# Conditional residual layer on one core: the first transfers, the slot table, the bias tiles and two weight loads change places

## The reference

```
selected_W = W[cat_ids]
selected_b = b[cat_ids]
out = x + jnp.einsum('bsd,bdh->bsh', x, selected_W) + selected_b[:, None, :]
```

## Time and profile before

| | |
|---|---|
| median of three executions | 99.44 us (99.01 to 99.58) |
| the profiled execution, its own time | 99.07 us |
| its span, first to last instruction | 97.1 us |
| granted TensorE clock | 1.00 |
| busy: TensorE / VectorE / ScalarE / GpSimd | 88% / 55% / 57% / 36% |
| moved by DMA | 31.25 MB, mean 322 GB/s |

### The profile page before, as it was taken

How to read it: one execution, slowest core, us unless ns; L and a number is a source line. 1 busy time by engine, 2 the same in 40 slices (tenths; PEclk the granted TensorE clock), 3 DMA queues, 4 the chain that set the end, 5 groups by cost and what they waited for, 6 DMA issues and landing times.

```text
span 97.1 us, 3027 instructions
## 1 busy us (share of the span) xinstructions
PE 85.9 (88%) x788; PEld 57.8 (60%) x788; DVE 53.8 (55%) x130; ACT 55.3 (57%) x98; POOL 34.6 (36%) x65
## 2 busy tenths in 40 slices
PE   0319969999999699999999999999999999999980
PEld 0107736666766375666766676757575767676640
DVE  2792407648255376739293657575566555464840
ACT  1403195592447464977758653976766768585500
POOL 5400000000000039999895655786307560000000
DMA  0999999999999999999999999999997899995363
GB/s 13 240 373 350 347 351 348 349 345 347 347 348 349 347 348 361 346 346 322 397 361 402 371 402 373 395 392 361 386 370 263 203 372 351 354 338 174 121 203 108
DMA packets 19970, 31.25 MB, mean 322 GB/s; under 512 B 1521, under 2 KB 15986, under 8 KB 19954
## 3 DMA queue, kind: packets, MB, share of 16 engines
q0 software_dynamic: 4640, 16.26, 46.6%
q1 hardware_dynamic: 13602, 13.18, 42.3%
q10 hardware_dynamic: 1712, 1.64, 5.7%
HBM read 25.30 MB, written 8.39 MB: 347 GB/s over the span
## 4 chain that ended last, share of the span: by engine, by line
PE 62%; ACT 1%; DVE 0%; issue 0%; ACTq 0%; SPq 0%
PE mm_ps L594 42%; PE xt_ps L505 12%; PE mm_ps L580 7%; PE xt_ps L594 2%; ACT w_slot L335 1%; DVE rows L475 0%; PE xt_ps L580 0%; ACTq L335 0%; SPq L206 0%
## 5 line engine op out<-in xcount | busy, mean ns | idle before, releaser
L594 PE MATMUL mm_ps<-w_slot,xT 128*64 128x256 f32 x496 | 57.2, 380 | 2.0 <-ACT w_slot L335 1.9
L335 ACT COPY w_slot<-w_all 128x512 f32 x64 | 38.4, 619 | 28.7 <-POOLq L206 8.8
L594 PEld LDWEIGHTS mm_ps<-w_slot,xT 128*64 128x64 f32 x496 | 34.5, 137 | 18.8 <-issue 1.9
L475 DVE TENSOR_TENSOR rows<-mm_ps,rows 128x512 f32<-128x512 f32 (+1 forms) x32 | 21.5, 673 | 24.8 <-PE mm_ps L594 24.5
L335 DVE COPY w_slot<-w_all 128x512 f32 x64 | 27.4, 458 | 7.6 <-SPq L206 3.9
L190 POOL DMA_DIRECT2D w_all<-in_L_cond_W x32 | 16.4, 515 | 37.7 <-DMA w_all<-in_L_cond_W 31.8
L505 PE MATMUL xt_ps<-ident,rows 128*128 128x128 f32 x128 | 18.8, 293 | 2.1 <-DMA rows<-in_x 2.1
L347 ACT COPY xT<-xt_ps 128x512 f32<-128x512 f32 x32 | 17.1, 584 | 5.3 <-PE xt_ps L505 5.3
L505 PEld LDWEIGHTS xt_ps<-ident,rows 128*128 128x128 f32 x128 | 14.8, 149 | 7.8 <-issue 5.2
L580 PE MATMUL mm_ps<-bias_parts,is_sample 96*64 96x256 bf16 x124 | 9.9, 278 | 0.0
L213 POOL DMA_DIRECT2D rows<-in_x x9 | 7.7, 853 | 4.9 <-DMA out<-rows 3.9
(11 more groups left out here) (53 smaller groups left out, 12.5 us busy)
## 6 DMA issues: line engine op xcount, KB each, us to landing
w_all<-in_L_cond_W POOLq DMA_DIRECT2D x32, 256.0 KB
w_all<-in_L_cond_W SPq DMA_DIRECT2D x29, 256.0 KB, 5.7
out<-rows POOLq DMA_DIRECT2D x11, 512.0 KB, 7.5
rows<-in_x POOLq DMA_DIRECT2D x9, 512.0 KB, 6.9
rows<-in_x SPq DMA_DIRECT2D x6, 512.0 KB, 6.7
out<-rows SPq DMA_DIRECT2D x8, 256.0 KB, 4.5
w_all<-in_L_cond_W ACTq DMA_DIRECT2D x3, 256.0 KB, 5.3
rows<-in_x ACTq DMA_DIRECT2D x1, 512.0 KB, 4.5
```

Source lines behind the costliest of these rows:

```text
L335: copy(w_slot[:, PAIR * p + half, :, :].rearrange("p k h -> p (k h)"), w_all[:, bass.ds(c, 1), :, :].rearrange("p c k h -> p (c k h)")).th ...
L475: V.tensor_tensor(to, sums, to, ALU.add).then_inc(sums_added, 1)
L594: last = T.matmul(to[HALF * half:HALF * (half + 1), :], xT[:, slot, k, j, :], w_slot[:, j, k, :], start=False, stop=(k == K - 1), skip_gro ...
```

## The change

ScalarE issues the rows of group 0 as its first transfer, ahead of its half of the bias; SP issues the rows of group 1 where it issued those of group 0. VectorE copies `slot_words` ahead of the three masks of the bias. On ScalarE the wait for `plan_read` 2 and the reading of group 0's slots stand ahead of the two weight loads, which are now 4 and 7 (SP issues 6); the slots of group 1 are read after the third weight copy, and `xT` of group 1 is copied one half behind each of the first two weight copies. TensorE makes one bias tile behind each of the first three pairs, and VectorE waits for one tile at a time; ahead of the last tile TensorE waits until three tiles are copied out.

```diff
-ACT_LOADS = (0, 6, 7)
+ACT_LOADS = (0, 4, 7)
@@ sync
             sp.dma_start(bias_nat[0:C, :], bias).then_inc(bias_loaded, 16)
-            load_rows(sp, 0)
+            load_rows(sp, 1)
             load_rows(sp, 2)
@@ scalar
+            load_rows(act, 0)
             act.dma_start(bias_nat[C:PAIR * C, :], bias).then_inc(bias_loaded, 16)
-            load_rows(act, 1)
...
             for k in range(K):
                 x_half(0, k)
+
+            act.wait_ge(plan_read, 2)
+            slots = slots_of(mybir.EngineType.Activation, 0, 1)
             for n in ACT_LOADS[1:]:
                 load_weights(act, n, part(word, n % WORD))
-
-            act.wait_ge(plan_read, 2)
-            slots = slots_of(mybir.EngineType.Activation, 0, 1)
...
                 now = slots
-                if g + 1 < GROUPS:
+                if 0 < g < GROUPS - 1:
                     slots = slots_of(mybir.EngineType.Activation, g + 1, 1)
                 for p in range(PAIRS_IN_GROUP):
                     copy_weights(act, nc.scalar.copy, now[p], g, p, 1, odd_weights_ready)
-                    if g == 0 and p == 1:
-
-                        for k in range(K):
-                            x_half(1, k)
+                    if g == 0 and p < K:
+
+                        x_half(1, p)
+                    elif g == 0 and p == K:
+                        slots = slots_of(mybir.EngineType.Activation, 1, 1)
@@ vector
+            dve.wait_ge(plan_products, 4)
+            V.tensor_copy(slot_words[:, :], slot_words_ps).then_inc(plan_read, 1)
+
             dve.wait_ge(masks_set, 2)
...
             assert steps[0] == PLAN_STEPS["bias"]
-            dve.wait_ge(plan_products, 4)
-            V.tensor_copy(slot_words[:, :], slot_words_ps).then_inc(plan_read, 1)
             dve.wait_ge(plan_read, 2)
...
-                    dve.wait_ge(tiles_made, 1 if p == 1 else TILES - 1)
+                    dve.wait_ge(tiles_made, p)
                     put_tile(p)
@@ tensor
-                    if g == 0 and pair == 0:
-
-                        for n in range(1, TILES):
-                            bias_of_tile(n).then_inc(tiles_made, 1)
+                    if g == 0 and pair + 1 < TILES:
+
+                        if pair + 1 == TILES - 1:
+
+                            pe.wait_ge(bias_ready, TILES - 1)
+                        bias_of_tile(pair + 1).then_inc(tiles_made, 1)
```

## The result

The changed kernel took 100.16 us in the median of six executions (99.79 to 100.48), the kernel before 99.38 us beside it (six, 99.01 to 99.74). The ratio is 1.0075, with a 95% interval of 1.0043 to 1.0108: slower by 0.75%. The forecast was 99.35 and no change. The profiled execution took 100.33 us, its span is 98.2 (99.07 and 97.1 before). Executions some 1.5% or more above the fastest of their kernel are left out of every median and ratio (in e3 three of twelve, 101.9 to 102.4, elsewhere at most two).

What follows compares the result with a forecast made beforehand. SP's report of load 25 and load 31's landing were taken to bound the kernel. Report +0.08 and the last pair at 0.86 gave -0.15, taken as -0.1: 99.44 - 0.1, rounded to 99.35, range 98.85 to 99.85.

Steps and rivals of the forecast that it cites:

- two things that fix the end: End of group 4: SP's report of load 25 at 32.87 and load 31's landing at 38.13 together set it.
- the exchange of the rows: Start of transfers: rows 0 on ScalarE land at about 5.7 instead of 7.5; the 512 KB issue starts 0.59 earlier.
- the stream: DMA transfers from the start: engines fill earlier, gain 0.3 us, bounds 0 and 0.59, so load 31 lands 0.3 earlier.
- SP's run: SP's unbroken issues from 5.88 to its report of load 25: one step longer, report 0.08 later.
- The ALU step: SP's issue of load 6 instead of 4: one more step to extract its category, about 0.08.
- the sum: Report 0.08 later, group 4's last pair no longer held by load 31: -0.15 to 0, taken as -0.1.
- The first stage: TensorE's group 0: transposes about 1.8 earlier, first pair at about 11.2 instead of 13.05; later waits absorb the gain.
- Loads 4 and 7: Issued by ScalarE, with SP issuing 6: SP's run grows by one ALU step, about 0.08; same bytes.
- The late categories: Start of queues: ScalarE's 512 KB get ahead of the categories, delaying plan and SP's loads; priced +0.9, chance 0.12.
- The slower rival: Categories land later behind ScalarE's 512 KB, delaying SP's first load and last report: 100.3 us, chance 0.12.
- The rule of packets in turn: DMA engines take queues in turn, a packet at a time, so the categories would wait one packet at most.

Runs made afterwards that it cites:

- e3: Kernel before, with ScalarE issuing the rows of group 1 ahead of its bias half and no exchange of groups: 100.06 us, ratio 1.0051.
- e1: Kernel before, with only the start of transfers changed: ScalarE issues rows of group 0, then its bias half, SP rows of group 1: 99.88 us, ratio 1.0027.
- e5: Changed kernel, with ScalarE issuing its bias half ahead of the rows of group 0: 99.63 us, ratio 1.0038.
- e8: Changed kernel, with loads 24 and 25 reported by GpSimd instead of SP: 100.05 us, ratio 1.0065.
- e9: Changed kernel, with eight more transposes filling TensorE's idle time before bias tile 0: 100.04 us, ratio 1.0117.
- e13: Changed kernel, with ScalarE's first issue held until the categories have landed: 101.28 us, ratio 1.0155.
- e15: Changed kernel, with both bias halves on SP ahead of its rows and none on ScalarE: 99.34 us, ratio 0.9978.
- e7: Changed kernel without ScalarE's bias half; GpSimd sets those 64 partitions to zero: 99.89 us, ratio 1.0055.
- e4: Kernel before, with rows of groups 0 and 1 exchanged between SP and ScalarE, bias half still first on ScalarE: 99.61 us, ratio 1.0016.
- e10: Kernel before, with ScalarE's part alone: loads 4 and 7 for 6 and 7, slots read ahead, group 1's xT copies moved: 99.59 us, ratio 1.0039.
- e12: Kernel before, unchanged, timed and profiled once more: 99.26 us, ratio 1.0011.
- e14: Changed kernel, with SP's bias half also behind its two transfers of rows: 101.11 us, ratio 1.0164.
- e6: Changed kernel, with ScalarE's bias half read from x instead of the bias, same order, size and shape: 100.37 us, ratio 1.0084.
- e11: Kernel before, with only the slot table ahead of the masks and one bias tile behind each of three pairs: 99.35 us, ratio 1.0016.
- e2: Changed kernel, with the start of transfers as in the kernel before, all other edits kept: 99.73 us, ratio 1.0029.

## Why the prediction was wrong

**The frame was right but for one limit.** The prediction named two things that fix the end, SP's report of load 25 and the landing of load 31; the profiles show a third, TensorE's own first stage. These three can hold the start of group 6's transposes, after which TensorE only works: SP's report of load 25 plus 6.94 (from the chain before: 39.81 - 32.87), the landing of load 31 plus 1.92 (40.03 - 38.11), and group 2's transposes plus four groups of 5.04, which is 20.16. Where TensorE stops once ahead of group 1's pairs (in the changed kernel 0.26 at 21.08, for VectorE's weights), that takes 0.47 more. The latest of the three is the measured start in every profile:

```
kernel   group 2   report 25  load 31   latest of the three     measured
before   18.24     32.87      38.11     40.03 (load 31)         40.03
after    19.17     34.23      39.22     41.17 (report)          41.17
e1       21.10     33.40      38.56     41.26 (TensorE)         41.24
e3       19.49     33.86      39.18     41.10 (load 31)         41.10
e5       17.88     32.99      38.49     40.41 (load 31)         40.41
e8       19.84     33.5       39.39     41.31 (load 31)         41.31
e9       18.20     33.37      38.78     40.70 (load 31)         40.70
e13      21.98     33.52      39.26     42.61 (TensorE, +0.47)  42.60
e15      17.72     33.16      38.72     40.64 (load 31)         40.64
```

The other profiles agree to 0.1 as well. In the changed kernel the report and the landing (39.22 + 1.92 = 41.14) lie 0.03 apart, so e8 could gain nothing. VectorE's last step starts 54.4 later in the profiles before and after.

**The step that failed: the exchange of the rows.** The prediction gave the stream a gain of 0.3 with bounds 0 and 0.59, "since the bytes are the same". The bytes do come at the same rate (347 and 348 GB/s from 7.4 to 37.4), and the start's gain of 227 KB was measured and given back by 7.4. What sets load 31 is its last part, forecast 0.3 earlier and measured 1.1 later. The lower bound of 0 excluded a loss on the strength of a mean over 16 engines. e15 shows that the loss hangs on the start of the transfers: with the 64 KB moved and nothing else it is gone. e3 and e5 point to the order of the 64 KB and the 512 KB on ScalarE's queue, e7 and e15 say that it is not this order alone: with nothing behind the rows the loss is there in one and gone in the other, and what differs in the transfers is 64 KB more ahead of SP's rows. The exchange of the two groups by itself costs nothing that can be told (e1, e4).

How the start reaches load 31 is shown only in part. The last part's landing, against the kernel before:

```
kernel   spread  load 13  load 17  load 21  load 31
before    0.9     19.51    24.51    29.08    38.11
after     3.6     +1.26    +1.63    +1.54    +1.11
e1        2.5     +1.16    +0.60    +0.52    +0.44
e8        2.0     +0.64    +0.13    +1.38    +1.28
e4        1.1     +0.28    +0.80    +1.16    +1.00
e10       0.3     +0.22    +0.76    +0.68    +0.59
e15       1.2     +0.35    +0.71    +0.66    +0.61
e12       1.1     +0.13    -0.26    +0.31    +0.33
```

Up to load 13 the start is what counts: the seven kernels with a spread of 2.0 or more (in e3 that of SP's first rows) are 0.6 to 1.3 behind there, the others 0.35 at most (but for e13 and e14, over 1.0). Between loads 13 and 21 parts fall behind or catch up again in every profile, the unchanged kernel's too (e12's distance from first to last part goes from 1.0 to 1.9), and at load 31 the two kinds overlap: 0.44 to 1.29 behind and 0.19 to 1.00. What happens there no run shows.

**SP's run: 0.08 forecast, 1.36 measured.** The ALU step was right (0.10). The rest are the long issues. That they are a consequence of the parts left behind is argued, not shown. For it: in all 17 profiles the last part of load 31 landed 6.0 to 6.8 after its issue, as if SP were held to that distance, while its first part took 2.9 in the changed kernel and 4.8 before; so the last part's 6.0 is more than a late issue asks for. Against it: after, e3, e4 and e6 each have an issue of 1.1 to 1.2 with load 31 after 39.0, but e11 has one of 1.3 (26.52) with load 31 at 38.3, and e12 one of 1.1. Either way it was not a step of the sum, which took pauses as chance.

**The first stage: 1.8 us earlier forecast, 0.26 measured, then 0.9 lost.** Rows 0 were there in time (transposes at 5.36). The bias came later than forecast: VectorE began its work on it at 6.23 rather than 5.3 to 5.8, and `slot_words` was copied at 8.00, after the 7.79 of before and not at 7.1 to 7.6. Load 1 landed at 11.86 and not at 10.2. Above all the prediction gave TensorE's early work its later durations: it named no cost for idle time between transposes and bias tile. e9 shows one, near 1 us at group 2's transposes. The granted clock stands at 1.00 in all these rows, so the trace doesn't call it the clock; the durations (1.97 against 1.09 for eight transposes of the same shape) are those of about half the pace. The Trainium skill, "TensorE: Matmul & The Clock Gate", section "What's actually happening", describes an engine that starts at 1.2 GHz, reaches 2.4 GHz after sustained work and falls back when idle; the durations agree with that, the granted clock of the rows does not show it. This slack is small: TensorE is 1.6 us from setting the end (18.24 + 20.16 against 40.03). In e1 it did, in e13 and e14 by far.

**Loads 4 and 7.** Forecast as nothing but the ALU step. e10, which has them with the moved slots and `xT`, gives +0.4% with a wide interval (1.0004 to 1.0075), e2 and e5, with the tiles as well, 0.3% and 0.4%. But e15 has all of it and is 0.2% under the kernel before. Whether this part costs anything is open.

**The rivals.** The late categories did not happen: `cats` was converted at 2.15 and SP's first load issued at 5.87, as before. The slower rival was priced at 100.3, and 100.16 was measured, but by another mechanism at the start of the same queues: that the number is near is luck. The rule of packets in turn that the prediction cites from the Trainium skill, "DMA: Bandwidth & Descriptors", section "Queues, rings and completion order", agrees with what was seen of the categories. It is hard to square with load 0 in the trace of the kernel before: from 5.5 to 7 us the queue of the rows of group 2 moved 0.55 MB and the other, on which load 0 had waited since 3.09, 5 packets of 1 KB or less. The measurement decides: load 0 was served in order of issue, as the prediction read it. Two smaller readings of the prediction were off: ScalarE's first two issues ended at 1.92 and not at 2.09, and load 0 was issued at 3.34 and not at 3.09.

**What stays open.** Why 512 KB first on ScalarE's queue leave single parts behind. They do in after, e1, e3, e6, e7, e8 and e9 (spreads 2.0 to 3.6; e3's on the rows SP issued first), with a bias half behind them or not (e7), whatever it reads (e6). They don't in e15, where SP's rows start 0.6 later, behind 128 KB, and not for the same transfer in e14, where nothing small lies between; e13, with ScalarE's rows 1.3 later, is in between (1.7). The part of each edit in the 0.75% is not separated either: the single parts measure 0.2 to 0.5% with intervals as wide.

## What to carry to other kernels

Bound a reordering of transfers by the last part of the transfer that is waited for, not by bytes and mean rate: at the same GB/s the last part of load 31 landed 1.1 us later. Take more than one profile before a step of 0.5 us is read as the edit's: two profiles of the kernel before differ by 0.3 at load 31. Write down all the limits that lie within 1 to 2 us of each other (here three within 1.6) and check each edit against every one of them, since earliness helps only the one in front and a loss counts on any. An early start of TensorE is worth little if it then idles: with 1.91 idle group 2's transposes came at 19.17, with the gap filled at 18.20, with 1.45 idle (e15) at 17.72.

## What the hardware showed that was not expected

The 16 parts of one transfer landed up to 3.6 us apart (rows of group 1, 5.93 to 9.54). The distance keeps for many loads and then changes in steps: 2.7 for loads 8 to 13, 2.4 at load 15, 3.5 for loads 16 to 25; in the kernel before 0.9 up to load 13 and 1.5 from load 15 on. An idle time of 1.9 us on TensorE behind 2 us of work kept the work from 10.0 to 14.7 at about half the pace (transposes and first pair 1.97 and 1.98, against 1.53 and 1.08 with the gap filled). Single issues of SP took up to 1.3 us where 0.38 is usual, in the kernel before as well (0.79 and 1.11 in its two profiles).
